# MLP halves behind the last head, and low-rank products in two row tiles, in a four-layer kernel on one core

## The reference

```python
# mixer: five token-dependent mixing vectors through a low-rank product
t = jnp.tanh(xxx @ maa_w1).reshape(B, L, 5, -1)          # 256 -> 5 x 32
m = jnp.einsum('blfd,fdc->blfc', t, maa_w2)              # 5 x (32 -> 256)
xw, xk, xv, xr, xg = (xa + sx * (maa_f + m_f) for each f)
# layer 3
hidden = out @ cproj_w + cproj_b + residual
y = jax.nn.gelu(layer_norm(hidden, ln2_w, ln2_b) @ fc_w + fc_b, approximate=True)
return hidden + y @ proj_w + proj_b
```

## Time and profile before

| what | value |
|---|---|
| median of three executions | 1226.01 us |
| profiled execution | 1226.18 us, of which the span from first to last instruction 1224.3 us |
| TensorE (PE) busy | 1108.3 us, 91% |
| VectorE (DVE) busy | 839.5 us, 69% |
| ScalarE (ACT) busy | 501.6 us, 41% |
| GpSimd (POOL) busy | 99.2 us, 8% |
| mean granted clock of TensorE | 0.933 of full speed |

### The profile page before, as it was taken

How to read it: one execution, slowest core, us unless ns; L and a number is a source line. 1 busy time by engine, 2 the same in 40 slices (tenths; PEclk the granted TensorE clock), 3 DMA queues, 4 the chain that set the end, 5 groups by cost and what they waited for, 6 DMA issues and landing times.

```text
span 1224.3 us, 14170 instructions
## 1 busy us (share of the span) xinstructions
PE 1108.3 (91%) x5312; PEld 746.4 (61%) x5312; DVE 839.5 (69%) x1142; ACT 501.6 (41%) x1543; POOL 99.2 (8%) x92
## 2 busy tenths in 40 slices
PE   6858989899889999987999989999999999999888
PEld 4634647556665666664766666665766666666665
DVE  5697689756986689779885589536895378942220
ACT  1003226622573135711574254433544326443741
POOL 1021010001010011001010011000110001100000
PEclk9978889989898889998999889999999999999899
DMA  9100000000000000000000000000000000000000
GB/s 369 51 1 0 1 27 5 1 1 26 6 1 1 18 9 6 1 0 19 13 1 1 26 5 1 1 18 26 5 1 1 18 27 5 1 3 14 14 1 18
DMA packets 13894, 22.64 MB, mean 18 GB/s; under 512 B 3841, under 2 KB 10625, under 8 KB 13186
## 3 DMA queue, kind: packets, MB, share of 16 engines
q1 hardware_dynamic: 13826, 21.74, 5.3%
HBM read 16.48 MB, written 2.10 MB: 15 GB/s over the span
## 4 chain that ended last, share of the span: by engine, by line
PE 63%; DVE 24%; ACT 7%; issue 3%; POOL 1%; DMA 1%; SPq 0%; DVEq 0%; ACTq 0%; POOLq 0%
DVE S_ L571 8%; PE PA L1165 7%; PE PB L1198 5%; PE QA L1373 5%; PE PB L1052 5%; PE QA L1052 4%; PE PA L1102 4%; ACT big L972 4%; DVE A L579 3%; PE QB L1285 3%; PE QB L1039 3%; DVE A L465 3%; DVE nmax L664 2%; PE QA L1301 2%; PE QA L1039 2%
## 5 line engine op out<-in xcount | busy, mean ns | idle before, releaser
L972 ACT ACTIVATE big<-QB,nmax 128x128 f32<-128x128 f32 x512 | 181.4, 376 | 104.9 <-DVE nmax L664 104.6
L1198 PE MATMUL PB<-A,common_w 128*128 128x256 f32 x512 | 136.3, 411 | 22.2 <-DVE A L579 22.1
L571 DVE TENSOR_TENSOR_SCAN S_<-W_,A 128x1024 f32<-128x1024 f32 x64 | 155.4, 2444 | 0.2
L1198 PEld LDWEIGHTS PB<-A,common_w 128*128 128x128 f32 x512 | 100.8, 208 | 44.0 <-DVE A L579 27.2
L664 DVE TENSOR_REDUCE nmax<-QB 128x4 f32<-128x512 f32 x128 | 86.9, 684 | 57.2 <-PE QB L1285 40.5
L972 ACT ACTIVATION_READ_ACCUMULATOR big<-QB,nmax 128x1 f32 x512 | 110.2, 215 | 0.0
L1165 PE MATMUL PA<-rwkv_w,X 128*128 128x256 f32 x384 | 100.3, 419 | 9.1 <-DVE X L435 9.0
L1285 PE MATMUL QB<-big,QX 128*128 128x256 f32 x384 | 100.1, 383 | 0.0
L1165 PEld LDWEIGHTS PA<-rwkv_w,X 128*128 128x128 f32 x384 | 80.3, 213 | 29.6 <-DVE X L435 11.6
L1301 PE MATMUL QA<-common_w,big 128*128 128x128 f32 x512 | 82.4, 285 | 15.1 <-ACT XT L981 8.0
L425 DVE SCALAR_TENSOR_TENSOR PA<-PA,rwkv_w,SX 128x512 f32<-128x512 f32 x80 | 58.7, 755 | 45.4 <-PE PA L1102 43.0
(11 more groups left out here) (180 smaller groups left out, 1778.0 us busy)
## 6 DMA issues: line engine op xcount, KB each, us to landing
rwkv_w<-in_rwkv_w SPq DMA_DIRECT2D x2, 2674.0 KB, 13.7
QX<-big SPq DMA_DIRECT2D x96, 32.0 KB, 1.9
attn_w<-in_attn_w SPq DMA_DIRECT2D x2, 1031.5 KB, 15.9
mlp_w<-in_mlp_w SPq DMA_DIRECT2D x1, 2052.0 KB, 23.5
X<-in_x SPq DMA_DIRECT2D x4, 512.0 KB, 13.3
ctx<-in_ctx SPq DMA_DIRECT2D x4, 512.0 KB, 3.4
ctx<-in_ctx_t SPq DMA_DIRECT2D x4, 512.0 KB, 3.5
...
```

What stands on the lines that cost most here:

```text
L571: last = v.tensor_tensor_scan(S_[:, d].rearrange("p k t -> p (k t)"), W_[:].rearrange("p k t -> p (k t)"), A_[c % 2][:, d].rearrange("p k ...
L972: last = s.activation(PR[:, n % 2, j], bank(2 + n % 2)[:, j * T:(j + 1) * T], ACT.Exp, bias=nmax[:, n % 2, j:j + 1], accum_out=den[:, b, h ...
L1198: last = t.matmul(y, ident, A_[c % 2][:, :, k], start=(c % 2 == 0 and k == 0), stop=False, skip_group_check=True)
```

## The change

1. **Low-rank products.** `maa` (after: line 1202) now issues four matmuls of 256 columns instead of two of 512: first, for channel half h, tokens' half q = h, then, behind a wait of TensorE for its own first pair (`r_pair`), the other two. The two of a pair read different groups of 32 rows of `low` and write different banks. For this `w1` holds seven column blocks (mixes 0 1 2 3 0 1 4): the tokens' second half is computed from columns 64 onward, so that mix f lies two row groups further on (line 1241: four matmuls of 256 columns instead of two of 512), and `w2r` is `w2a` rotated alike. The fifth mix is computed as eight matmuls of 128 columns, 32 array columns wide, one position per sequence (line 1246), and multiplied back in four pairs of 128 columns with a wait between pairs (`maa_last`, line 1216).
2. **MLP in halves.** In `attn_mlp` the MLP behind the second norm is done for sequences 2 and 3 only, with 256 columns. Sequences 0 and 1 of all four groups get a program of their own, `first_mlp`, that stands in chain H behind the last head on every engine, and uses the head's buffers (`PA`, `XN`, `X5`). It can start for a group once `a_x0` says that x of sequences 0 and 1 is updated.
3. **Output projection.** `output(0)` stands behind job 10 instead of behind all jobs; it writes bank 1, and the values of sequence 2, which use that bank, wait for the update of x (`a_x0`).
4. **Fill** in the last attention unit is dropped, and with it that unit's wait for the last gate.
5. The order strings are new, `mrow8` is one buffer instead of four and is loaded unit by unit, a few small buffers share room, outputs are stored by halves.

```diff
-RWKV_COLS = [("w1", HALF * NMIX * MIX), ("w2a", C), ("w2b", C), ("dw1", HALF * DEC), ("dw2", C),
+RWKV_COLS = [("w1", HALF * 7 * MIX), ("w2a", C), ("w2r", C), ("w2b", C), ("dw1", HALF * DEC), ("dw2", C),
...
     def maa(f, ready):
         for h in range(HALF):
             ready(h)
-            rows = MIX * f % P if f < 4 else P - MIX
-            w2 = r_(L, "w2a" if f < 4 else "w2b")[rows:rows + MIX, h * P:(h + 1) * P]
-            tt = (low if f < 4 else thT)[rows:rows + MIX]
-            t.matmul(pa(h), w2, tt, start=True, stop=True, tile_position=(rows, 0)).then_inc(sem["r_maa"], 1)
+        for k in range(2):
+            if k:
+                yield
+                pe.wait_ge(sem["r_pair"], u.at("r_pair", 2 * f + 2))
+            for h in range(HALF):
+                q = (h + k) % 2
+                rows = MIX * ((f + 2 * q) % 4)
+                w2 = r_(L, "w2r" if q else "w2a")[rows:rows + MIX, h * P:(h + 1) * P]
+                last = t.matmul(pa(h)[:, 256 * q:256 * q + 256], w2, low[rows:rows + MIX, 256 * q:256 * q + 256],
+                                start=True, stop=True, tile_position=(rows, 0))
+                last.then_inc(sem["r_maa" if k else "r_pair"], 1)
+    def maa_last(f, ready):
+        for h in range(HALF):
+            ready(h)
+        for k in range(4):
+            if k:
+                yield
+                pe.wait_ge(sem["r_pair"], u.at("r_pair", 8 + 2 * k))
+            for h in range(HALF):
+                q = (h + k) % 4
+                rows = slice(MIX * q, MIX * q + MIX)
+                last = t.matmul(pa(h)[:, T * q:T * q + T], r_(L, "w2b")[rows, h * P:(h + 1) * P], low5[rows],
+                                start=True, stop=True, tile_position=(MIX * q, 0))
+                last.then_inc(sem["r_maa" if k == 3 else "r_pair"], 1)
...
     for h in range(HALF):
         mixed(0)(h)
-        t.matmul(PA[:, 0:512], w1[:, h, 0:P], flat(X5[0])[:, h], start=(h == 0), stop=(h == 1))
-    yield
-    for h in range(HALF):
-        last = t.matmul(PA[P - MIX:P, 512:1024], w1[:, h, P:P + MIX], flat(X5[0])[:, h], start=(h == 0), stop=(h == 1),
-                        tile_position=(0, P - MIX))
+        for q in range(2):
+            t.matmul(PA[:, 256 * q:256 * q + 256], w1[:, h, 64 * q:64 * q + P], flat(X5[0])[:, h, 256 * q:256 * q + 256],
+                     start=(h == 0 and q == 0), stop=(h == 1), skip_group_check=True)
+    yield
+    for h in range(HALF):
+        for q in range(4):
+            last = t.matmul(PA[MIX * q:MIX * q + MIX, 512:512 + T], w1[:, h, 6 * MIX:7 * MIX],
+                            flat(X5[0])[:, h, T * q:T * q + T], start=(h == 0), stop=(h == 1), tile_position=(0, MIX * q))
     last.then_inc(sem["r_used"], 1)
     fill(4)
     yield
-    maa(0, lambda h: pe.wait_ge(sem["r_lowrank"], u.at("r_lowrank", h + 1)))
+    yield from maa(0, lambda h: pe.wait_ge(sem["r_lowrank"], u.at("r_lowrank", h + 1)))
...
+    yield from maa_last(4, turned(3))
...
     def values(b):
         pe.wait_ge(sem["a_pc"], u.at("a_pc", QUAD * (b + 1)))
-        if b and b % 2 == 0:
-            pe.wait_ge(sem["a_on"], u.at("a_on", b // 2))
+        if b == 2:
+            pe.wait_ge(sem["a_x0"], u.at("a_x0", 1))
...
+    def output(k):
+        pe.wait_ge(sem["a_on"], u.at("a_on", k + 1))
+        token_pair(bank(1), ah_(L, "Wo"), lambda h, b: CT[:, h, b * T:(b + 1) * T], k, lambda h: None,
+                   1 if mlp else None, 2 * k).then_inc(sem["a_o"], 1)
...
+        if n == 10:
+            yield
+            output(0)
+    yield
+    output(1)
...
-        fill(24)
...
+        turn_two(lambda h: bank(2 + h), az, 2, sem["a_xT"])
         for m in range(FFT):
+            if m % 2 == 0:
+                yield
+            fc_two(bank(m // 2)[:, 256 * (m % 2):256 * (m % 2) + 256], m, halves_xt,
+                   lambda h: pe.wait_ge(sem["a_xc"], u.at("a_xc", h + 3)), sem["a_fc"])
+        for b in range(2):
+            yield
+            proj_one(QA[:, 512 + b * C:512 + (b + 1) * C], lambda m: H_[:, m, b * T:(b + 1) * T],
+                     lambda k: pe.wait_ge(sem["a_gelu"], u.at("a_gelu", max(k + 1, 2))), b, sem["a_mlp"])
+def first_mlp(u):
+    yield
+    pe.wait_ge(sem["m_z"], u.at("m_z", 1))
+    turn_two(lambda h: PA[:, 512 * h:512 * h + 256], z, 0, sem["m_xT"])
+    for m in range(FFT):
+        if m % 2 == 0:
             yield
             if m >= 4:
-                pe.wait_ge(sem["a_gelu"], u.at("a_gelu", m - 3))
-            for h in range(HALF):
-                if m == 0:
-                    pe.wait_ge(sem["a_xc"], u.at("a_xc", h + 3))
-                last = t.matmul(bank(m % 4), fc[:, h, m * P:(m + 1) * P], XT[:, h], start=(h == 0), stop=(h == 1))
-            last.then_inc(sem["a_fc"], 1)
-        proj = m_("proj").rearrange("p (m n) -> p m n", m=FFT)
...
+def fc_two(o, m, src, ready, done):
+    fc = m_("fc").rearrange("p (h n) -> p h n", h=HALF)
+    for h in range(HALF):
+        if m == 0:
+            ready(h)
+        last = t.matmul(o, fc[:, h, m * P:(m + 1) * P], src[:, h], start=(h == 0), stop=(h == 1))
+    if m % 2:
+        last.then_inc(done, 1)
+def proj_one(o, lhs, ready, b, done):
+    proj = m_("proj").rearrange("p (m n) -> p m n", m=FFT)
+    for m in range(FFT):
+        if b == 0 and m % 2 == 0:
+            ready(m // 2)
+        t.matmul(o, lhs(m), proj[:, m], start=(m == 0), stop=False)
+    last = add_bias(o, 2)
+    if b:
+        last.then_inc(done, 1)
...
+    def update(k):
         dve.wait_ge(sem["a_o"], u.at("a_o", k + 1))
         part = slice(512 * k, 512 * k + 512)
         if mlp:
-            last = v.tensor_tensor(xf[:, part], QA[:, part], xf[:, part], ALU.add)
-        else:
-            last = v.scalar_tensor_tensor(xf[:, part], QA[:, part], tanh_gate[:, 0:1], xf[:, part], ALU.mult, ALU.add)
-    last.then_inc(lane_sem["x_done"][u.lane], 1)
+            return v.tensor_tensor(xf[:, part], bank(1), xf[:, part], ALU.add)
+        return v.scalar_tensor_tensor(xf[:, part], bank(1), tanh_gate[:, 0:1], xf[:, part], ALU.mult, ALU.add)
...
+            yield
+            x_ready(u, 0 if mlp else 1)
+            update(0).then_inc(sem["a_x0"], 1)
...
+def first_mlp(u):
+    X = X2[u.lane]
+    xf = X[:].rearrange("p b c -> p (b c)")
+    yield
+    dve.wait_ge(sem["a_x0"], ATTENTIONS[G + u.group].at("a_x0", 1))
+    norm_stats(X, bn, mv, sem["m_stats"], (0, 1))
+    yield
+    dve.wait_ge(sem["m_rstd"], u.at("m_rstd", 1))
+    norm_apply(z, X, mv, rstd, sem["m_z"], (0, 1))
+    yield
+    dve.wait_ge(sem["m_mlp"], u.at("m_mlp", 1))
+    v.tensor_tensor(m_out[u.index], PA[:, 0:512], xf[:, 0:512], ALU.add).then_inc(sem["m_out"], 1)
```

260 lines of the change are left out of this document (144 added, 116 removed).

## The result

The changed kernel takes **1204.4 us** (median of four executions, 1203.6 to 1209.0), the kernel before, run beside it, 1227.3 (four executions, 1220.3 to 1228.6). The ratio is 0.983, 95% interval 0.980 to 0.986. The forecast was 1196 us, in a range of 1170 to 1220: faster, as forecast, and inside the range, but a quarter of the forecast gain (30 us, 22 came) is missing. The profiled execution took 1204.0 us, its span 1202.2.

A forecast was written before the change was run, and what follows sets the result against it. TensorE, busy 91%, was taken to bound most but not all of the time. From 1226.2 us, -13 (to the fifth mixer), -42 (to the eighth), +24 (the rest) and +1 (start) gave 1196 us, range 1170 to 1220.

The forecast's parts named there:

- To 596.3 us: First stretch, to the fifth mixer: 16.2 us less TensorE work gives 10 us, the clock 3 us, together -13 us.
- I let 0.6 through, 10 us: First stretch: 0.6 of the 16.2 us TensorE saving shortens the time, VectorE being busy 77 to 84% there.
- Overlap of pairs: Low-rank products: matmuls in different row groups overlap fully, so 34.4 us are saved over eight heads.
- Price of the waits between pairs: TensorE waiting for its own pair: 0.25 us at 36 waits, 0.19 at 20 with another piece between, 12.8 us in all.
- A saving of TensorE's time and not of the head's chain: Low-rank products: VectorE gets its first bank 1.27 us after the product's start, where it was 0.86 + 0.16.
- Fifth mix: Line 1127: two matmuls of 512 columns (1.72 us) become eight narrow ones (0.51 us), saving 9.7 us for eight heads.
- Second stretch: Fifth to eighth mixer: 58 us less TensorE work, 1 us costing 0.54 us of time; 423 against 465 us, -42.
- Last part: After the eighth mixer: work +30, clock -5, filled waits -2, function tables +1, together +24 us.
- B: Whole kernel: TensorE sets the pace throughout, so all savings count, 1181 us; chance 0.22.
- C: Low-rank products: the pairs do not overlap, 34.4 us come back, 1222 us; chance 0.08.
- E: Up to the last head: VectorE's chain sets the time, TensorE's saving turns into waiting, 1251 us; chance 0.07.
- D: Second stretch: VectorE holds it in part, only 20 us of 58 come through, 1218 us; chance 0.11.

The follow-up runs named there:

- kernel 1: Changed kernel with the low-rank part of the kernel before (two matmuls of 512 columns per product, fifth mix as before): 1218.3 us, ratio 0.993 to 0.997.
- kernel 2: Kernel before with only the new low-rank part, plus shared small buffers and the mask row loaded unit by unit, old order strings: 1225.1 us, ratio 0.998 to 1.003.
- kernel 8: Changed kernel with both matmuls of a pair in the same group of 32 rows, so that they cannot overlap: 1234.2 us, ratio 1.005 to 1.009.
- kernel 6: Changed kernel with banks by halves of the tokens, so no TensorE wait for itself between a product's pairs: 1220.3 us, ratio 0.994 to 0.998.
- kernel 5: Changed kernel with the pairs of each product joined, no piece of another program between them: 1213.5 us, ratio 0.986 to 0.992.
- Kernel 4: Changed kernel with the fifth mix as before (two matmuls of 512 columns each way), other four mixes in pairs: 1216.3 us, ratio 0.990 to 0.995.
- kernel 10: Changed kernel without the 128 mask products of the attention jobs, about 28 us less TensorE work: 1193.5 us, ratio 0.974 to 0.978.

## Why the prediction came out as it did

| stretch | forecast | low-rank part | all the rest | measured |
|---|---|---|---|---|
| to mixer 5 | -13 (+1 for the start) | -8.6 | +7.7 | -0.9 |
| to mixer 8 | -42 | -2.6 | -44.1 | -46.7 |
| the last part | +24 | -1.5 | +27.0 | +25.5 |

The low-rank column is the changed kernel less kernel 1, the rest is kernel 1 less before. Taken in the other order, by kernel 2, the low-rank part is +4.7, -7.6 and 0.1, and the rest -5.6, -39.1 and +25.4; only the sums hold in both.

- **The step that failed** is the sum "To 596.3 us". It counts the low-rank work and the clock, and puts at nothing, without a reason, what the new order and buffers do in that stretch. By kernel 1 that term is +7.7 us with the same TensorE and VectorE work. The clock's "3 us" did not come (0.90 before and after). "I let 0.6 through, 10 us" came out at 8.6 us of 16.2 (0.53), and the masks taken out of the changed kernel give 0.50 there, so beside the new order this size was near. It is not a property of the stretch, though: in the old order the masks give 0.19, and kernel 2 has no gain there. So 1.4 us are missing in the slope, 3 in the clock, 7.7 in the term left out, together 12 of the -13; the first stretch moved by -0.9, and the 1 us for the start, forecast on top, is in the 7.7.
- **What that 7.7 us is** stays open. The early output projection is not it (it brings 5 of the other sign), nor more work on TensorE or VectorE; it is TensorE's idle time, spread over three mixers. Beside the new products the same rest brings 5.6 us, so 7.7 is its size beside the old ones only. What is left as a cause is the order of the pieces, which may suit the new products and not the old, and the shared buffers and mask loads; no run changed one of them at a time. Nor did a run take the MLP halves or the fill by themselves, so for the second stretch and the last part "the rest" is all that is shown.
- **Overlap of pairs: right**, fully (kernel 8). **Price of the waits between pairs**: forecast 0.25 us behind the own pair; measured, 1.49 us for a product that the forecast puts at 0.86 + 0.25 = 1.11. Every pair has 0.20 us beside its columns, and kernel 6 puts the wait itself at 0.31 (1.49 less 1.18). Against 1.91 us before, a product with its pairs together saves 0.42, a split one 0.65 (two times 0.63); 0.61 and 0.67 were forecast (1.72 less 1.11, and less 1.05). Over 32 products that is a few us, not the missing part.
- **"A saving of TensorE's time and not of the head's chain": right in sign, too kind in size.** The first bank was forecast 1.27 us after the start. It comes after 1.5 where the pairs stand together, and after 3.3 us where a piece of 2 us stands between, one of the 20 places that the forecast priced at 0.19 us of TensorE and at nothing for the chain. VectorE waits 15 us more for it in all than in kernel 1; but kernel 5, which takes 10 of these away, is slower, so this wait is not where the missing time went.
- **Fifth mix: right for its first product** (0.6 us against 1.72), **wrong for the last**: 2.2 us in four pairs, where half of the columns' 1.72 and three waits of 0.25 had given 1.6. Kernel 4 says that with both the fifth mix is most of what the low-rank part brings in all, but not in the first stretch.
- **Second stretch: right by luck, two errors that cancel.** The MLP halves and the order were given 37 us of work at 0.54 or more, and brought 44.1 beside the old products (39.1 beside the new); the low-rank part was given a share of 21.5 less 6.4 us and brought 2.6 (7.6 in the old order), though TensorE is busy 94% there. That a stretch shows TensorE at 94% did not make its savings count, there or in kernel 10 (0.15).
- **Last part: right** (188.2 + 1.8 outside of the span = 190 us, as forecast), with the clock at 1.00. Of its terms the tables are up to 3 us and not 1, and the low-rank part's 1.5 us were not in it.
- **Rivals.** B (all savings count, 1181) and C (1222) are out by kernels 10 and 8, E (slower, 1251) by the time itself. D's time in the second stretch did not come, but its idea, that most of a TensorE saving there does not count, holds for the low-rank part.

No kernel of these that computes the whole reference beats the changed one.

## What to carry to other kernels

A slope of time against one engine's work, read between stretches, is not a price; take a small piece of work out of the kernel (28 us here) and read what comes through: it was 17% in one order of these programs and 32 to 39% in the other. Where three engines play an order fixed by hand, price a change of the order as a term of its own, with both signs, because nearly the same edit was worth 0 us in one order and 14 in the other. And when a product is cut into parts that others run between, count for each reader when the last part it needs arrives, but test that this reader's wait is one that the time follows before acting on it.
